# Sharing out the adjacency scatters of a graph network kernel otherwise between its stages

## What is computed

```python
def _gatv2_layer(x, src, dst, Wl, bl, Wr, br, att, bias, heads, out_ch, concat):
    xl = (x @ Wl + bl).reshape(N, heads, out_ch)
    xr = (x @ Wr + br).reshape(N, heads, out_ch)
    e = jax.nn.leaky_relu(xl[src] + xr[dst], NEG_SLOPE)
    logits = jnp.einsum('ehc,hc->eh', e, att)
    m = jax.ops.segment_max(logits, dst, num_segments=N)
    ex = jnp.exp(logits - m[dst])
    denom = jax.ops.segment_sum(ex, dst, num_segments=N)
    msg = xl[src] * (ex / denom[dst])[..., None]
    return jax.ops.segment_sum(msg, dst, num_segments=N) + bias
...
x = x + L0(relu(layernorm(x)))   # two attention layers: 8 heads of 16, then 1 head of 64
x = x + L1(relu(layernorm(x)))   # one weighted graph convolution
x = x + L2(relu(layernorm(x)))   # edge features, segment sum, two batch norms
x = x + L3(relu(layernorm(x)))   # three weighted graph convolutions
```

## Time and profile before

| | us |
|---|---|
| median of 3 runs | 6715.57 (6712.33 to 6718.6) |
| the profiled execution, its time | 6720.51 |
| its span | 6718.6 |
| logits of layer 1, from its gathers to its barrier | up to 1317.3 |
| edge maxima of layer 1 | to 1429.3 |
| sums of layer 1 | to 1908.2 |
| end of layer 1 | to 1983.6 |
| edge maxima of layer 2 | 3120.5 to 3159.2 |
| sums of layer 2 | to 3570.2 |
| end of layer 2 | to 3664.6 |

### The profile page before, as it was taken

How to read it: one execution, slowest core, us unless ns; L and a number is a source line. 1 busy time by engine, 2 the same in 40 slices (tenths; PEclk the granted TensorE clock), 3 DMA queues, 4 the chain that set the end, 5 groups by cost and what they waited for, 6 DMA issues and landing times. The chain is left out here.

```text
span 6718.6 us, 98108 instructions
## 1 busy us (share of the span) xinstructions
PE 4849.3 (72%) x22735; PEld 3497.7 (52%) x22735; DVE 4075.3 (61%) x13068; ACT 2302.0 (34%) x5676; POOL 4529.0 (67%) x4354
## 2 busy tenths in 40 slices
PE   3677765237777666543886996666666799999998
PEld 2344443236664444332775996555555455555555
DVE  7898985589976676334887445444444644344343
ACT  4344444259953333333995003222222400000000
POOL 1777777778857777777886661777777177375473
PEclk9555555569965555555997998777777799999999
DMA  5988865457644444333444884655555299999998
GB/s 202 298 301 287 278 188 147 114 100 142 141 80 108 106 106 104 81 80 48 76 76 105 290 283 146 186 161 159 161 159 157 67 304 305 295 304 297 300 304 255
DMA packets 915215, 1226.12 MB, mean 182 GB/s; under 512 B 248092, under 2 KB 652720, under 8 KB 901674
## 3 DMA queue, kind: packets, MB, share of 16 engines
q1 hardware_dynamic: 593614, 879.21, 40.8%
q0 software_dynamic: 206208, 217.12, 16.7%
q10 hardware_dynamic: 114828, 123.48, 5.6%
HBM read 981.30 MB, written 239.21 MB: 182 GB/s over the span
## 5 line engine op out<-in xcount | busy, mean ns | idle before, releaser
L1180 POOL DMA_INDIRECT ACC<-table,TABS x1760 | 1665.7, 946 | 609.2 <-issue 609.2
L1495 POOL DMA_INDIRECT BUF<-table,TABS x840 | 797.6, 949 | 589.8 <-issue 244.7
L1261 POOL DMA_INDIRECT adjacency<-TABS x600 | 966.8, 1611 | 301.8 <-issue 264.7
L1801 POOL DMA_INDIRECT TABS<-table,SPOT_SRC x836 | 789.3, 944 | 317.9 <-issue 317.9
L1983 PE MATMUL picked<-BUF,G 128*128 x2368 | 596.1, 433 | 448.6 <-DVE ACC L2008 402.3
L1983 PEld LDWEIGHTS picked<-BUF,G 128*128 128x128 f32 x2368 | 526.2, 327 | 690.7 <-issue 690.7
L2379 PE MATMUL asum<-BUF 128*128 128x144 f32 x3520 | 561.6, 305 | 166.3 <-DVE BUF L2357 163.4
L1991 DVE TENSOR_TENSOR picked<-picked,ACC 128x512 f32<-128x512 f32 (+1 forms) x440 | 247.6, 563 | 574.1 <-DMA ACC<-table,TABS 503.0
L1824 PE MATMUL pre<-wmat,BUF 128*128 128x128 f32 x1672 | 321.2, 352 | 358.5 <-DVE BUF L1850 346.2
L2379 PEld LDWEIGHTS asum<-BUF 128*128 128x128 f32 x3520 | 476.8, 197 | 197.2 <-issue 184.3
L2325 ACT ACTIVATE BUF<-iota_row,TABS 128x128 f32<-128x128 f32 x1760 | 555.2, 386 | 22.6 <-PEq L98 22.6
(11 more groups left out here) (449 smaller groups left out, 9783.9 us busy)
## 6 DMA issues: line engine op xcount, KB each, us to landing
TABS<-adjacency SPq DMA_DIRECT2D x272, 512.0 KB
BUF<-in_edge_pair SPq DMA_DIRECT2D x836, 128.0 KB
BUF<-adjacency SPq DMA_DIRECT2D x102, 1024.0 KB
BUF<-adjacency SPq DMA_DIRECT2D x204, 512.0 KB
adjacency<-zeros ACTq DMA_DIRECT2D x44, 1792.0 KB
G<-adjacency SPq DMA_DIRECT2D x136, 512.0 KB
kept<-ACC SPq DMA_DIRECT2D x220, 272.0 KB, 3.7
G<-kept SPq DMA_DIRECT2D x220, 272.0 KB
```

What stands on the lines that cost most here:

```text
L1180: po.indirect_dma_start(rows[:, slot, j, 0:width], None, tab, bass.IndirectOffsetOnAxis(ap=SRC[:, q * GT + j:q * GT + j + 1], axis=0)).the ...
L1261: po.indirect_dma_start(adj_flat, bass.IndirectOffsetOnAxis(ap=PLACE[:, k:k + 1], axis=0), TOTAL[:, k:k + 1], None, compute_op=ALU.add).th ...
L1495: po.indirect_dma_start(R[:, q % deep_ring, j, :], None, table, bass.IndirectOffsetOnAxis(ap=SRC[:, k:k + 1], axis=0)).then_inc(S(f"gather ...
L1801: po.indirect_dma_start(R[:, g % RD, j, :], None, table, bass.IndirectOffsetOnAxis(ap=SPOT_SRC[:, k:k + 1], axis=0)).then_inc(S(f"gathered ...
```

## The change

Of the 150 groups, the same 80 and 70 are sent in the two layers, in the same order, but by another share of the stages: one group in each logit tail in place of four, the same 11 and 4 beside the edge maxima, 61 and 54 in the sums in place of 56 and 52, and 7 and 11 at the layers' ends in place of 9 and 10.

```diff
-MERGES = ((4, 11, 56, 9), (4, 4, 52, 10))
+MERGES = ((1, 11, 61, 7), (1, 4, 54, 11))
```

## The result

The changed kernel took 6668.28 us (median of 4 runs, 6665.56 to 6671.13) against 6715.59 us before (4 runs). The ratio is 0.9927, 95% interval 0.9914 to 0.9940: 47 us, or 0.7%, less. The forecast was 6667.6 us.

What follows compares the result with a forecast made beforehand. POOL's scatters alone were taken to bound the logit tails, with free time in the sums; -26.1 - 22.4 + 2.0 + 0.6 - 2.1 = -48.0 us from the median 6715.6 gave 6667.6 us, range 6655 to 6684.

Steps and rivals of the forecast that it cites:

- The reading of the tails: Logit ends: POOL alone bounds them; after the change SP is last or equal in layer 1, POOL last in layer 2.
- Part 1 and 2: Logit tails of layers 1 and 2, twelve scatters fewer in each: -26.1 us and -22.4 us.
- signs of being wrong: Scatters in the sums stepping clearly above 1.9 us, tail lag past 7.4, or a different time after the attention network.
- Part 3: Sums of layer 1, twenty scatters more: POOL's drain, with lag 7.4, ends after DVE's arrival, +2.0 us.
- Part 4: Sums of layer 2, eight scatters more: with lag 5.6 +0.6 us, between 0 and +2.8.
- Part 5: Sums: more scatters do not slow the other engines, 0 us, with 2.7 us kept as the bound.
- Part 6 and 7: Layer ends: eight scatters fewer in layer 1, SP late next, -2.1 us; four more in layer 2, hidden by SP, 0.
- Part 8: Edge maxima of both layers: the same 44 and 16 scatters, 0 us.
- the fear of +5.4: Edge maxima of layer 2: POOL's lag may be 7.4 instead of 2.0, +5.4 us, a bound only.
- A backlog of gathers that hides the tails: Rival, logit tails: the drain waits for gathers, not scatters, so no change, 6716 us; chance 0.04.
- Scatters stalled by VectorE: Rival, sums: moved scatters cost 3.89 us each beside VectorE, slower than before, 6723 us; chance 0.02.
- The clock: Rival: shorter pauses leave TensorE's clock lower in a later stage, losing 18 us, 6686 us; chance 0.07.

Runs made afterwards that it cites:

- the overfilled one: Against the changed kernel, five more groups in layer 1's sums (66) and four more in layer 2's (58), taken from the layers' ends: 6726.13 us, ratio 1.0017.

## Why the prediction was right

**The reading of the tails** was right: SP was late next in layer 1 within 0.7 us, in layer 2 POOL itself, 6.5 us behind SP (forecast 5.9). The run with the tails back shows that they carry the gain.

**Part 1 and 2**, -26.1 and -22.4, measured -25.8 and -21.7. Both were off by the lag, which was 7.6 and not 6.8. That lies outside the bounds of 2.0 to 7.4 that I had read from six stages; it cost 0.7 us in the first and 0.8 in the second: the lag after 880 gathers and four scatters isn't that after 880 and sixteen. Two of the prediction's own signs of being wrong came up: this lag past 7.4, and another time in the stages behind. The first moved the time by 0.8 us at most in a stage; the second comes with long tails and with short ones.

**Part 3** is the step that failed: +2.0, measured -1.1. What was mis-sized is the lag, "each stage keeps its own lag in the sum": it goes with the count since the last drain, and 244 lies just behind a fall, 2.2 us in place of 7.4. POOL was to be 2.0 us behind DVE and was 6.1 ahead, 8.1 us between them: 5.2 are the lag and 4.0 the pace of the scatters, less the 1.1 that DVE came earlier. With the old lag the stage would have been at the edge: in the changed kernel's first profile the last scatter ended at 1873.9, which with 7.4 is 1881.3 against DVE's 1882.2; in its second, where the scatters ended at 1876.8, it would have been 1884.2 against DVE's 1881.7, 2.5 us late, and POOL's drain ended at 1879.1 instead. The scatters themselves ran at 7.67 us a group in the first ((1873.9 - 1406.3) / 61) for the 7.73 of the forecast, which with their start makes the 4.0 us, and would alone have brought the forecast +2.0 to 0. The stage's own -1.1 us is DVE's, which reached the barrier 477.3 us after the one ahead instead of 478.4.

**Part 4**, +0.6, measured +0.9, with the lag of 216 scatters (6.3) for that of 208 (5.6), and 14.6 us for the two groups in place of 15.0. Its upper bound is mis-added in the prediction: 3564.6 + 7.4 - 3569.6 is +2.4, not +2.8. The lower end of the range is 2 us off in the same way: 6660 and the 3 us make 6657, not 6655. Neither touches the forecast.

**Part 5**, no slowing of the others, holds: DVE reached the barrier of layer 1's sums 477.3 us after the barrier ahead with 244 scatters, 475.9 with 264, 479.6 with 248 and 478.4 with 224, in no order with the count. In layer 2 it was 410.5 us in the kernel before (208 scatters), in the changed one (216) and in the overfilled one (232).

**Part 6 and 7**, -2.1 and 0, measured -2.1 and -0.2. In part 7 POOL came 2.3 us before SP, where 4 were to spare. **Part 8**, 0, with the lag of 2.0 kept at 2.0: the fear of +5.4 was unfounded, since the count in that stage didn't change.

**The rivals.** A backlog of gathers that hides the tails: out, by the run with the tails back. But it had a grain of truth, as the gathers have a lag of 7.2 without any scatter. Scatters stalled by VectorE: out in the sums, where 244 scatters took (1873.9 - 1406.3) / 244 = 1.92 us each. The trace of the kernel before shows, too, that the length of the DVE operation isn't all: in the edge maxima of layer 2 the three scatters from 3121.85 to 3129.22 us, which started beside operations of 3.4 us with two inputs, took 3.1 to 3.6 us, and the one at 3132.67, beside a reduction (one input) as long, took 1.57. The clock: the last convolutions took 1376 to 1384 us in all kernels timed, in no order with the pauses (1383.5 and 1376.6 with both pauses long, 1377.4 and 1380.4 in two profiles of the changed kernel, 1383.0 with the tails' groups at the layers' ends). No stage shows that anything was taken back.

**Luck.** That the median came within 0.7 us of the forecast is in part luck: the four runs span 5.6 us, and the errors of parts 1, 2 and 4 (+0.3, +0.7 and +0.3) go against that of part 3 (-3.1). The profiled pair, 55.5 us apart, has another 6.8 us in stages that the change doesn't touch.

## What to carry to other kernels

Read the barrier, not the busy shares: the drain that ends last names the engine that bounds a stage, and the distance to the next one is all that an edit to that engine's work alone can bring there. Work off the critical path is free up to the edge and costs its full price past it (five and four groups too many turned 0.7% less into 0.2% more), so budget it in time per stage, with the drain's lag counted in. Where items wait for each other's landing, leave one ahead of the barrier to start the chain.

## What the runs showed of the hardware that I had not expected

POOL's drain ends well after its last indirect DMA, by 1.7 to 9.1 us. The lag isn't a constant and doesn't belong to a stage: it grows by roughly 0.05 us with each scatter since the last drain (2.0 to 2.3 us at 16, 6.9 at 112), and falls back to 2 us at somewhere between 112 and 120 scatters and again between 224 and 232. Gathers behave in their own way: 880 of them leave 7.2 us, 880 and four scatters 7.6, 880 and sixteen 6.8, the same in both layers within 0.1 us. Behind the gathers of other stages, in all profiles, it was 5.9 to 6.4 us after 280, 5.6 to 6.3 after 836 and 6.7 to 7.9 after 840. What POOL does in that time no row shows, and it stays open. For a stage that POOL bounds, some 5 us can hang on the count, as between 112 and 120.
